# Attention over windows of three blocks: one query block's probabilities turned by VectorE and moved through DRAM

## What is computed

```python
xn = layernorm(x)                       # x: 8192 tokens x 512
q, k, v = split(xn @ Wqkv + bqkv)       # 16 heads of 32
# query block n (128 tokens) sees key blocks n-1, n, n+1
scores = einsum('bhnqd,bhnkd->bhnqk', qb, kwin) / sqrt(512)
scores = where(abs(kpos - qpos) <= 128, scores, -1e30)
out = einsum('bhnqk,bhnkd->bhnqd', softmax(scores), vwin)
y = x + (out @ Wout + bout) + ffn(xn)   # ffn: bit-linear layers with a low-rank term
```

## Time and profile before

| | us |
|---|---|
| runs (3), median | 2630.02 (2627.89 to 2631.48) |
| profiled execution | 2629.41 |
| its span | 2627.6 |
| TensorE busy | 2576.2 |
| ScalarE busy | 1638.1 |
| VectorE busy | 1592.0 |
| GpSimd busy | 631.8 |

### The profile page before, as it was taken

How to read it: one execution, slowest core, us unless ns; L and a number is a source line. 1 busy time by engine, 2 the same in 40 slices (tenths; PEclk the granted TensorE clock), 3 DMA queues, 4 the chain that set the end, 5 groups by cost and what they waited for, 6 DMA issues and landing times.

```text
span 2627.6 us, 55989 instructions
## 1 busy us (share of the span) xinstructions
PE 2576.2 (98%) x19728; PEld 2090.2 (80%) x19728; DVE 1592.0 (61%) x4779; ACT 1638.1 (62%) x4260; POOL 631.8 (24%) x595
## 2 busy tenths in 40 slices
PE   6999999999999999989999999999999999999998
PEld 4888888888888888868888888888888888888885
DVE  5444444444444444357777777777777777777775
ACT  6333333333333333358888888888888888888886
POOL 0011111111111111033333333333333333333332
PEclk7999999999999999999999999999999999999999
...
DMA packets 188361, 167.43 MB, mean 64 GB/s; under 512 B 11328, under 2 KB 143424, under 8 KB 187632
## 3 DMA queue, kind: packets, MB, share of 16 engines
...
q0 software_dynamic: 144, 0.17, 0.0%
...
## 4 chain that ended last, share of the span: by engine, by line
PE 55%; ACT 1%; issue 0%; DVE 0%; POOL 0%; POOLq 0%; ACTq 0%
PE pT_ps L1193 14%; PE job_ps L1105 14%; PE score_ps L1176 7%; PE job_ps L1123 7%; PE job_ps L1217 7%; PE job_ps L1114 7%; ACT wqkv_raw L928 1%; ACT wqkv_raw L938 0%; PE job_ps L1237 0%; PE score_ps L1227 0%; DVE wqkv_raw L1006 0%; DVE k_lo L1038 0%; ACT q_hi L954 0%; ACT k_hi L957 0%; POOL wout_raw L899 0%
## 5 line engine op out<-in xcount | busy, mean ns | idle before, releaser
L928 ACT ACTIVATE wqkv_raw<-wqkv_raw,neg_max 128x384 f32<-128x384 f32 (+1 forms) x1024 | 633.3, 619 | 186.3 <-DVE neg_max L1006 181.5
L888 POOL TENSOR_SCALAR wqkv_raw<-wqkv_raw,sum_rcp 128x384 f32<-128x384 f32 (+1 forms) x256 | 372.9, 1457 | 960.1 <-DVE sum_rcp L1017 960.1
L494 ACT ACTIVATE relu<-up_ps,fc_scale 128x512 f32<-128x512 f32 x256 | 176.2, 688 | 656.2 <-PE up_ps L625 656.2
L938 ACT COPY wqkv_raw<-pT_ps 128x384 f32<-128x384 f32 (+1 forms) x1024 | 484.7, 474 | 74.4 <-PE pT_ps L1193 74.1
L1193 PE MATMUL pT_ps<-ident,wqkv_raw 128*128 128x128 f32 x3040 | 513.4, 277 | 8.1 <-ACT wqkv_raw L938 7.7
L1006 DVE CUSTOM_DVE_ANT_0 wqkv_raw<-score_ps,mask 128x384 f32<-128x384 f32 (+1 forms) x1024 | 503.5, 548 | 5.7 <-PE score_ps L1176 1.6
L568 DVE SCALAR_TENSOR_TENSOR sq<-up_ps,relu 128x512 f32<-128x512 f32 x256 | 177.0, 692 | 531.8 <-ACT relu L494 530.4
L1193 PEld LDWEIGHTS pT_ps<-ident,wqkv_raw 128*128 128x128 f32 x3040 | 360.0, 140 | 119.1 <-ACT wqkv_raw L938 42.6
L635 PE MATMUL down_ps<-proj_T,sq_hi 128*128 128x512 f32 x1024 | 408.9, 399 | 0.9 <-DVE sq_lo L551 0.9
L637 PE MATMUL down_ps<-proj_T,sq_lo 128*128 128x512 f32 x1024 | 404.3, 395 | 0.0
L621 PE MATMUL up_ps<-f_xT_hi,fc_T 128*128 128x512 f32 x1024 | 399.2, 390 | 1.4 <-DVE low L539 1.4
(11 more groups left out here) (126 smaller groups left out, 4228.2 us busy)
## 6 DMA issues: line engine op xcount, KB each, us to landing
xT_hi<-xT SPq DMA_DIRECT2D x65, 256.0 KB, 3.8
xT_lo<-xT SPq DMA_DIRECT2D x65, 256.0 KB, 4.5
f_x_in<-in_L_attn_x SPq DMA_DIRECT2D x64, 256.0 KB, 3.2
xT<-f_xT_hi SPq DMA_DIRECT2D x64, 256.0 KB, 2.6
xT<-f_xT_lo SPq DMA_DIRECT2D x64, 256.0 KB, 2.8
part_in<-in_L_attn_x SPq DMA_DIRECT2D x64, 256.0 KB, 3.4
partial<-f_y SPq DMA_DIRECT2D x64, 256.0 KB, 2.0
wout_raw<-partial SPq DMA_DIRECT2D x64, 256.0 KB, 2.8
```

The lines of the kernel that those rows point to most:

```text
L888: nc.gpsimd.tensor_scalar(probs[:, u, cols], probs[:, u, cols], sum_rcp[:, u:u + 1], None, ALU.mult).then_inc(last_head_normalised, 1)
L928: nc.scalar.activation(probs[:, u, cols], probs[:, u, cols], ACT.Exp, bias=neg_max[:, u:u + 1], scale=-1.0, accum_out=prob_sum[:, u:u + 1] ...
L938: nc.scalar.copy(pT[:, h, first + seen.start:first + seen.stop, :].rearrange("p w t -> p (w t)"), pT_ps[:, h % 2, seen.start * P:seen.stop ...
```

## The change

For query block b=0, TensorE no longer turns the probabilities. ScalarE scales heads 0 and 1, VectorE head 2, GpSimd head 3, after one reciprocal for all four. VectorE turns each head in 32x32 pieces (`turn_blocks`, L1102 of the changed kernel) into `blocks`, where a row holds all four heads of 32 queries (512 bytes). SyncE writes `blocks` to DRAM in one DMA (`move_blocks_out`) and reads it back in four (`move_blocks_in`), which bring each piece of 32 keys to its partitions: `pT_moved`. In the four steps of i = 0 there are four DMAs out. Block b=1 is turned by TensorE as before.

TensorE does job B ahead of the value product, and the banks' order follows. VectorE takes the maxima of b=1 after q_lo and k_lo as before, then normalises b=1, then `oT_low`. ScalarE does the four exps of b=1 in a row and then `oT_high`. The value product is 24 products of 128 columns in place of 8 of 256 and 8 of 128. `values` has five blocks in place of six, `oT_hi` and `oT_lo` six chunks in place of eight.

```diff
-    VR = 6
+    VR = 5
     XR = 3
+    OR = 6
+    STRIPS = P // DH
...
-        pT = wqkv_raw[:, 2:4, :].rearrange("p a (h w k) -> p (a h) w k", w=6, k=P)
...
+        blocks = sb("blocks", [P, STRIPS, 3, HC, DH], F32)
+        pT_moved = wqkv_raw[:, 2, :].rearrange("p (w q h t) -> p w q h t", q=STRIPS, h=HC, t=DH)
+        pT = wqkv_raw[:, 3, :].rearrange("p (h w k) -> p h w k", w=3, k=P)
+        oT_hi = sb("oT_hi", [P, OR, T], F32R)
+        oT_lo = sb("oT_lo", [P, OR, T], F32R)
...
-            return (3 * (t + 1) + 1) % 2
+            return (3 * (t + 1) + 2) % 2
...
         def b_bank(t):
-            return (3 * t + 2) % 2
+            return (3 * t + 1) % 2
...
-            if k == 1:
+            if k == 2:
...
+            def move_blocks_out(t):
+                i, _ = where(t)
+                first = blocks_seen(i, 0).start
+                moved = turned_dram[t % 2 * STRIPS:(t % 2 + 1) * STRIPS, :, :, :]
+                sp.wait_ge(blocks_turned, HC * (t + 1))
+                if first == 0:
+                    sp.dma_start(moved.rearrange("a w p x -> p (a w) x"),
+                                 blocks.rearrange("p a w h t -> p (a w) (h t)")).then_inc(blocks_out, 16)
...
+            def move_blocks_in(t):
+                i, _ = where(t)
+                first = blocks_seen(i, 0).start
+                sp.wait_ge(blocks_out, 16 * transfers_out(t + 1))
+                if t >= 1:
+                    sp.wait_ge(pv_done, t)
+                for a in range(STRIPS):
+                    moved = turned_dram[t % 2 * STRIPS + a, first:3, :, :].rearrange("w (q j) x -> j (w q) x", j=DH)
+                    sp.dma_start(pT_moved[a * DH:(a + 1) * DH, first:3, :, :, :].rearrange("j w q h t -> j (w q) (h t)"),
+                                 moved).then_inc(blocks_moved, 16)
...
+            for t in range(STEPS + DC):
+                i, c = where(t)
+                if t < STEPS:
+                    move_blocks_out(t)
+                    move_blocks_in(t)
+                if c == 1 and i + XR - 1 < NT:
                     load_x(i + XR - 1)
+                if c >= 2 and i >= 1:
+                    store_y(i - 1, c - 2)
+                    if i < NT:
+                        load_part(i, c - 2)
...
+            def normalise_moved_head(t):
...
+                pool.wait_ge(rcp_done, 3 * t + 1)
+                nc.gpsimd.tensor_scalar(probs[:, u, cols], probs[:, u, cols], sum_rcp[:, u:u + 1], None, ALU.mult
+                                        ).then_inc(pool_head_normalised, 1)
...
+                cols = window(i, 0)
+                act.wait_ge(rcp_done, 3 * t + 1)
+                for u in range(HC // 2):
+                    nc.scalar.mul(probs[:, u, cols], probs[:, u, cols], sum_rcp[:, u:u + 1]
+                                  ).then_inc(act_heads_normalised, 1)
...
                 act.wait_ge(pv_done, t + 1)
-                if i >= 2 and c == 0:
-                    act.wait_ge(job_filled, B_NUMBER[4 * (i - 1) + 2])
-                nc.scalar.copy(oT_hi[:, i % 2, c, :], job_ps[:, pv_bank(t), 0:T]).then_inc(oT_hi_done, 1)
+                if i >= 1 and c == OR - DC:
+                    act.wait_ge(job_filled, B_NUMBER[4 * i + 2])
+                nc.scalar.copy(oT_hi[:, t % OR, :], job_ps[:, pv_bank(t), 0:T]).then_inc(oT_hi_done, 1)
...
+                        copy_pT(t - 1, h)
                     if t < STEPS:
                         exp(t, 0, h)
+                if t < STEPS:
+                    normalise_first_heads(t)
                 if job_a(t) is not None:
                     qk_high(job_a(t), A_NUMBER[t], a_bank(t))
                 for h in range(HC):
                     if t < STEPS:
                         exp(t, 1, h)
-                    if h == 0 and 1 <= t <= STEPS:
-                        oT_high(t - 1)
-                    if t < STEPS:
-                        copy_pT(t, 0, h)
+                if 1 <= t <= STEPS:
+                    oT_high(t - 1)
...
-                if t >= 1:
-                    dve.wait_ge(turned, 8 * (t - 1) + HC * (b + 1))
+                if t >= 1 and b == 0:
+                    dve.wait_ge(blocks_turned, HC * t)
+                if t >= 1 and b == 1:
+                    dve.wait_ge(turned, HC * t)
...
+            def inverse_sums(t, first, count):
+                heads = slice(first, first + count)
+                dve.wait_ge(exped, 8 * t + first + count)
+                nc.vector.reciprocal(sum_rcp[:, heads], prob_sum[:, heads]).then_inc(rcp_done, 1)
...
+            def normalise_moved_head(t):
...
+                inverse_sums(t, 0, HC)
+                dve.wait_ge(rcp_done, 3 * t + 1)
+                nc.vector.tensor_scalar(probs[:, u, cols], probs[:, u, cols], sum_rcp[:, u:u + 1], None, ALU.mult
+                                        ).then_inc(dve_head_normalised, 1)
...
+            def normalise(t, pair):
...
+            def turn_blocks(t, u):
+                i, _ = where(t)
+                seen = blocks_seen(i, 0)
+                if u < HC // 2:
+                    dve.wait_ge(act_heads_normalised, HC // 2 * t + u + 1)
+                elif u == HC - 2:
+                    dve.wait_ge(dve_head_normalised, t + 1)
+                    if t >= 1:
+                        dve.wait_ge(blocks_out, 16 * transfers_out(t))
+                else:
+                    dve.wait_ge(pool_head_normalised, t + 1)
+                nc.vector.transpose(blocks[:, :, seen.start:seen.stop, u, :].rearrange("p a w t -> p w a t"),
+                                    probs[:, u, seen.start * P:seen.stop * P].rearrange("p (w a t) -> p w a t", a=STRIPS, t=DH)
+                                    ).then_inc(blocks_turned, 1)
...
                     add_out(b[1], b[2], B_NUMBER[t - 1], b_bank(t - 1))
                 if t < STEPS:
                     find_max(t, 0)
-                    normalise(t, 0)
+                    normalise_moved_head(t)
+                    for u in (2, 0, 1, 3):
+                        turn_blocks(t, u)
                 if job_a(t) is not None:
                     qk_low(job_a(t), a_bank(t))
                 if t < STEPS:
                     find_max(t, 1)
+                if t < STEPS:
+                    for pair in range(2):
+                        normalise(t, pair)
                 if 1 <= t <= STEPS:
                     oT_low(t - 1)
-                if t < STEPS:
...
+                pe.wait_ge(blocks_moved, 16 * STRIPS * (t + 1))
+                pe.wait_ge(pT_done, HC * (t + 1))
+                for b in range(2):
+                    seen = blocks_seen(i, b)
+                    for w in seen:
+                        blk = 2 * i - 1 + b + w
+                        for h in range(HC):
+                            head = c * HC + h
+                            strip = slice(h * DH, (h + 1) * DH)
+                            cols = slice(at(i, b) * P, (at(i, b) + 1) * P)
+                            out_ = job_ps[strip, bank, cols].rearrange("p (q t) -> p q t", t=DH)
+                            p = pT[:, h, w, :].rearrange("p (q t) -> p q t", t=DH) if b else pT_moved[:, w, :, h, :]
+                            last = nc.tensor.matmul(out_, values[:, blk % VR, head * DH:(head + 1) * DH], p,
+                                                    start=(w == seen.start), stop=(w == seen.stop - 1),
+                                                    tile_position=(0, h * DH))
                 last.then_inc(pv_done, 1)
...
@@ -1254,16 +1337,14 @@
                     scores(t, 0)
                 for part in range(QUARTERS):
                     if 1 <= t <= STEPS:
-                        turn_probs(t - 1, 1, part)
+                        turn_probs(t - 1, part)
                     run_a(t, part)
                 if t < STEPS:
                     scores(t, 1)
+                for part in range(QUARTERS):
+                    run_b(t, part)
                 if 1 <= t <= STEPS:
                     probs_times_values(t - 1)
-                for part in range(QUARTERS):
-                    if t < STEPS:
-                        turn_probs(t, 0, part)
-                    run_b(t, part)
...
+    turned_dram = nc.dram_tensor("turned_blocks", [2 * (P // DH), 3, P, HC * DH], F32, kind="Internal").ap()
```

More of the change, by code:

```diff
@@ L769, in blocks_seen, with transfers_out @@
             return range(0 if 2 * i - 1 + b >= 0 else 1, 3 if 2 * i + 1 + b < NBLK else 2)
+        def transfers_out(steps):
+            return steps + (STRIPS - 1) * min(steps, DC)
         def job_a(t):
@@ L1008, in find_max @@
                                                    accum_out=neg_max[:, u:u + 1]).then_inc(maxed, 1)
-            def normalise(t, b):
-                i, _ = where(t)
-                cols = window(i, b)
-                for pair in range(2):
-                    first = b * HC + 2 * pair
-                    heads = slice(first, first + 2)
-                    dve.wait_ge(exped, 8 * t + first + 2)
```

(46 more changed lines are left out.)

72 lines of the change are left out of this document (36 added, 36 removed).

## The result

The change takes 2762.82 us, the median of 4 runs (2762.12 to 2764.17), against 2628.95 for the kernel before (4 runs, 2627.36 to 2631.48). The ratio is 1.0509, with an interval of 1.0491 to 1.0527: slower by 5.1%, or 133.9 us. The prediction was 2768.

A forecast was written before the change was run, and what follows sets the result against it. TensorE bounds the kernel before, the VectorE-ScalarE softmax loop after: 12.2 us plus 0.3 for clock falls, 12.5 against 11.44 over 126 steps, 134 plus 4 on 2629.4, giving 2768 as median; range 2680 to 2880.

The forecast's parts named there:

- first maximum to the reciprocal of b=0: VectorE's first maximum of a step to the end of the fourth exp of b=0: 4.26 us.
- falls of the clock: TensorE idling before job A halves its granted clock: 1.3 us in one step in four, 0.3 us a step.
- What bounds: TensorE bounds the 128 attention steps before; afterwards the softmax loop of VectorE and ScalarE sets the step, 12.2 us against 11.44.
- TensorE's own work: TensorE's work in an attention step without the four turns of b=0: 11.44 - 1.47 = 9.97 us.
- x: Time of one 128x384 turn on VectorE: taken as 0.50 us, bounded by 0.33 and 0.95.
- 4x on the path: All four VectorE turns of b=0 add to the loop: 10.09 us plus 4x, 12.09 in all.
- TensorE's saving is kept: Rival: loop under 11.44 us with x under 0.34, so faster; 2586 at x = 0.25; chance 0.05.
- The pace behind job A: Job A waits for job B's bank behind an addition, so turns and copies of b=1 come late: 0.1 us.
- The sum: Whole run: (12.5 - 11.44) x 126 full steps = 134, plus 4, on 2629.4 us gives 2767.
- The detour: Turned blocks' DRAM round trip, 12.2 us within 13.0 available: nothing in a full step, 4 us once at the end.
- late transfers: Rival: a DRAM round trip of 16 us adds 1.5 us to each step, 2956; of 15 us, 2830; chance 0.10.
- The value product: TensorE's product, now 24 instructions of 128 columns, the same 3072 columns: kept at 1.44 us, or 2.16 by instructions.

The follow-up runs named there:

- e8: Change with VectorE taking b=0 by pairs, addition behind maxima of b=1, oT_low behind maxima of b=0, two b=1 turns ahead of job A: 2510.73 us.
- e2: Change with VectorE turning only head 2 from step 8 on; heads 0, 1 and 3 scaled but not turned: 2700.72 us.
- e5: Change with TensorE turning heads 0 and 1 of b=1 ahead of job A's first quarter: 2690.49 us.
- e3: Change with twelve extra 128-column TensorE products ahead of job A in steps behind an output job: 2725.22 us.
- e1: Change without the moves of turned blocks to DRAM and back and without the two waits for them: 2755.56 us.

## Why the prediction was right, step by step

The terms of the loop, as predicted and as the timelines above give them (us):

| term | predicted | measured |
|---|---|---|
| first maximum to the reciprocal of b=0 | 4.26 (+0.1 behind an addition) | 4.43, and 4.68 behind an addition |
| reciprocal, scaling, to the first turn | 0.66 | 0.67 |
| four turns | 2.00 | 1.89 |
| q_lo, k_lo | 0.79 | 0.75 |
| maximum to exp, exps to the reciprocal of b=1 | 3.20 | 3.12 |
| reciprocal, scaling, oT_low | 0.88 | 0.87 |
| addition, in half of the steps | 0.60 | 0.60 |
| **step, mean without falls** | 12.2 | 12.16 |
| falls of the clock, spread over all steps | 0.3 | 0.31 |

- **What bounds** was right: TensorE's own work no longer counted, and the loop between VectorE and ScalarE set the step. That work, though, was put too low at 9.97 us. In e8 TensorE is busy 1083 of 1100 us at a mean step of 10.45, so 10.3 a step, and in the change it is busy 87.5% of the stretch from 1300 to 2600 us (1137.75 of 1300), where I had said that the profile would show less than 85%.
- **x**, the price that no row showed, came out at 0.47 us (1.89 / 4) in a row of four, against 0.50 taken, 0.33 and 0.95 as bounds. One alone lasts 0.58, as a maximum nearly does (0.55). The Trainium skill (Vector Engine (DVE) Microarchitecture Reference, section 3.8) has the transposing front end sustain one element per cycle per lane; with the clock of "VectorE: DVE Perf Modes" that is an estimate of 0.40 us. The measured 0.47 is longer, and the measurement decides.
- **"4x on the path"** was right for the step's length but not as a slope. I had noted that ScalarE's scalings and q_hi and k_hi end beside the turns, and drew from it only that they cost nothing; they do stand 0.4 us behind (e2). So the rival "TensorE's saving is kept" could not have come true at any x: the step ends at the 11.32 and 12.25 of e2, 11.79 on average, above TensorE's former 11.44.
- **The pace behind job A** was the smallest term and the one most off: 0.1 in steps with an addition. It is 0.42 there (4.68 against 4.26) and 0.17 in all others, where I had none. In those, job A waits as well, 0.51 us at 1810.16, for ScalarE's `take_v` to empty the bank; I had looked at the steps with an addition alone. e5 shows that TensorE's order makes this term, not VectorE's. The sum came out right by some luck: the 4.26 was 0.30 short on average, and the 0.1, cheaper turns (0.11), exps (0.08) and q_lo and k_lo (0.04) made up for it. I had also put the 0.1 on every step, though only half of them hold an addition; by my own terms the loop was 12.14.
- **Falls of the clock**: one step in four at 1.3 us was predicted; 23 of 112 steps at 1.5 us is what the trace shows, and e3 took 37.6 us back by filling the idle time. All of them are in steps with an addition, where TensorE waits longest, as the prediction placed them (the 3.3 us before job A).
- **The detour** was rightly costed at nothing in a full step (e1), and at 4 us at the end, where it is 4.1. The round trip itself was priced too high. SyncE's timeline for the step above:

```profile
1805.63 0.37 SPq L865 DMA_DIRECT2D turned_blocks<-blocks  x1
...
1809.74 1.86 SPq L880 DMA_DIRECT2D wqkv_raw<-turned_blocks  x4
```

The way out takes 4.1 us (1805.63 to 1809.74, as the landing time on the profile's page says), where I had 5.6. The last of the four loads is issued at 1811.1 and lands 3.9 later, at 1815.0: 9.4 us in all against 12.2, and the value product that needs it starts at 1818.15. So "late transfers" did not come true, but in one step of the change only 1.08 us were left, because a load took 5.9 us to land.
- **The value product** took 1.52 us against 1.44 kept (48 records, two for each product, where before 16 products had 32). It lies beside the loop.
- **The sum.** Predicted 134 + 4; the profiled execution is 133.6 us above the one before. By the first maxima of the steps, 127.2 of that lie between the first step and the last, 1.02 in each of steps 8 to 120 against 1.06 predicted; 3.8 lie behind the last step's first maximum and 2.6 ahead of the attention stage, which the change does not touch.
